# Attention in halves of 256 queries instead of chunks of 512, with two slots of turned probabilities and rings of eight for their parts

## The reference

```python
x = x + layernorm(attention(layernorm(x)))
# attention, per head h, weights = codes * scales (one scale per 32 rows):
q, k, v = xn @ Wq + bq, xn @ Wk + bk, xn @ Wv + bv      # [2048, 128] each
p = softmax(q @ k.T / sqrt(128))                        # [2048, 2048]
out += (p @ v) @ Wo[h]                                  # + bo
x = x + layernorm(moe(layernorm(x)))                    # top 2 of 8, 176 hidden
```

## Time and profile before

| | us |
|---|---|
| median of 3 runs | 2824.37 (2823.85 to 2857.05) |
| profiled execution, its own time | 2834.33 |
| span of the profiled execution | 2832.5 |
| mean granted TensorE clock | 0.943 of full |

### The profile page before, as it was taken

How to read it: one execution, slowest core, us unless ns; L and a number is a source line. 1 busy time by engine, 2 the same in 40 slices (tenths; PEclk the granted TensorE clock), 3 DMA queues, 4 the chain that set the end, 5 groups by cost and what they waited for, 6 DMA issues and landing times.

```text
span 2832.5 us, 36223 instructions
## 1 busy us (share of the span) xinstructions
PE 2300.4 (81%) x10540; PEld 1812.0 (64%) x10540; DVE 1730.0 (61%) x2335; ACT 1389.5 (49%) x2492; POOL 1546.7 (55%) x1376
## 2 busy tenths in 40 slices
PE   4878787878788887878787878878787878855998
PEld 3667575756667666757575666657566657644876
DVE  4666666657566666666675756666666657645443
ACT  2454454545454555555454545544554545433332
POOL 1455556656565555565565656555556655554433
PEclk8999999989999999999999999999999999977999
DMA  4445454445454454555454645445455455470000
GB/s 75 112 109 118 105 126 112 112 107 134 102 125 109 111 126 105 117 126 118 105 121 110 135 103 124 113 108 117 105 126 120 112 116 120 113 180 11 8 8 15
DMA packets 152845, 298.68 MB, mean 105 GB/s; under 512 B 44896, under 2 KB 87264, under 8 KB 152800
## 3 DMA queue, kind: packets, MB, share of 16 engines
q1 hardware_dynamic: 152800, 298.11, 46.0%
HBM read 27.43 MB, written 2.10 MB: 10 GB/s over the span
## 4 chain that ended last, share of the span: by engine, by line
issue 41%; POOL 37%; PE 13%; DVE 4%; SPq 3%; DMA 2%; ACT 1%; POOLq 1%; ACTq 0%; DVEq 0%
POOL pT L393 33%; PE ps_s L488 2%; PE ps_s L489 2%; PE ps_s L490 2%; SPq L301 2%; POOL codes L382 1%; DVE part_max L1000 1%; DMA acc<-in_L_attn_bo 1%; PE ps_a L488 1%; PE ps_a L747 1%; DVE probs L1013 1%; PE ps_a L490 1%; PE ps_a L489 1%; PE ps_a L749 1%; PE ps_a L750 1%
## 5 line engine op out<-in xcount | busy, mean ns | idle before, releaser
L393 POOL TENSOR_TENSOR pT<-pT,pT_hi 128x512 fp32r<-128x512 f32 x1024 | 1298.4, 1289 | 975.5 <-ACT pT_hi L802 974.5
L791 ACT ACTIVATE probs<-ps_s,shift 128x1024 f32<-128x1024 f32 x512 | 569.2, 1112 | 777.6 <-DVE shift L1006 777.6
L488 PE MATMUL ps_a<-pT_hi,v_hi 128*128 128x512 f32 x1024 | 449.7, 439 | 408.3 <-POOL pT L393 408.2
L1000 DVE TENSOR_REDUCE part_max<-ps_s 128x1 f32<-128x1024 f32 x512 | 619.2, 1209 | 262.3 <-PE ps_s L490 261.2
L1013 DVE STREAM_TRANSPOSE probs<-probs 128x1024 f32<-128x1024 f32 x512 | 632.2, 1235 | 195.5 <-ACT probs L791 195.5
L802 ACT ACTIVATE pT_hi<-pT 128x512 fp32r<-128x512 f32 x1024 | 606.1, 626 | 76.1 <-DMA pT<-probs 55.1
L488 PEld LDWEIGHTS ps_a<-pT_hi,v_hi 128*128 128x128 f32 x1024 | 196.5, 192 | 559.6 <-POOL pT L393 526.4
L488 PE MATMUL ps_s<-kT_hi,qT_hi 128*128 128x512 f32 x1024 | 419.1, 409 | 9.1 <-ACT probs L791 6.6
L489 PE MATMUL ps_s<-kT_lo,qT_hi 128*128 128x512 f32 x1024 | 416.4, 407 | 0.0
L490 PE MATMUL ps_s<-kT_hi,qT_lo 128*128 128x512 f32 x1024 | 413.1, 403 | 0.0
L489 PE MATMUL ps_a<-pT,v_hi 128*128 128x512 f32 x1024 | 409.0, 399 | 0.0
(11 more groups left out here) (159 smaller groups left out, 2915.9 us busy)
## 6 DMA issues: line engine op xcount, KB each, us to landing
pT<-probs SPq DMA_DIRECT2D x2048, 128.0 KB, 2.4
probs<-in_L_attn_x SPq DMA_DIRECT2D x4, 512.0 KB, 5.3
codes<-in_L_attn_wk_codes SPq DMA_DIRECT2D x16, 128.0 KB, 2.2
scales<-in_L_attn_wk_scales SPq DMA_DIRECT2D x64, 32.0 KB, 2.8
acc<-in_L_attn_bo SPq DMA_DIRECT2D x1, 2048.0 KB, 31.2
codes<-in_L_attn_wo_codes SPq DMA_DIRECT2D x16, 128.0 KB, 2.1
scales<-in_L_attn_wo_scales SPq DMA_DIRECT2D x64, 32.0 KB, 1.8
x<-in_L_attn_x SPq DMA_DIRECT2D x4, 512.0 KB, 7.5
```

The lines of the kernel that those rows point to most:

```text
L393: pool.tensor_tensor(tile, full(tile), full(pT_hi[:, k % RING, :]).rearrange("p (i q) -> p i q", i=Q4), ALU.subtract).then_inc(sm["p_lo_do ...
L488: nc.tensor.matmul(dst, lhs_hi, rhs_hi, start=first, stop=False)
L791: nc.scalar.activation(out, src, ACT.Exp, bias=shift[:, j % 2, r:r + 1], scale=SCALE, accum_out=sums[:, j % 2, r, g:g + 1])\
L1000: V.tensor_reduce(part_max[:, j % 2, r, g:g + 1], ps_s[:, pair_of(j, NG2 * r + g), :], AX.X, ALU.max)\
```

## The change

- Chunks of 512 queries become halves of 256 (8 per head, s; HQ = 256, RH = 2 rows). probs still has two slots, now of one half each.
- pT gets two slots (s % 2), each with all 16 key tiles of a half, and is no longer written by POOL. Low parts go to a ring of their own, pT_lo; pT_hi and pT_lo have eight places of two key tiles of 256 queries each (RING = 8). A position is such a pair; high and low parts still are 128 x 512 operations, but the value products have 256 columns, twice as many. HI_LAG = 2, PV_LAG = 6, out of 8 positions.
- turn_blocks is one step per half: 16 DMAs of 128 KB, of 64 rows of 2 KB where there were 32 rows of 4 KB. It waits for p_turned of the whole half and for POOL's low parts of two halves before.
- qT has two slots; q_proj, out_proj and add_out work on 256 queries, output three iterations on. The small statistics have four slots.
- V is made in two pieces of 1024 in the score banks (pair 0), in iteration 1; K in two pieces of 1024, in pairs 0 and 1. ring_of says which pair a score use has; around V's pieces two pairs are left for the scores.
- The x, normed, comes in through pT instead of probs. The experts' weights and x1 are loaded after the last turning DMAs have landed. wr is loaded and split, and `before` made, at the start, on POOL; pick and combT are prepared on POOL after the first norm of the expert stage, not before.

The core of the diff (orders of the engines' programs in an iteration are given as they are after):

```diff
-    RING = 4
+    RING = 8
     PAIRS = 3
-    USES = TPC * NG2
-    PV_LAG = 12
-    HI_LAG = 10
+    USES = RH * NG2
+    PV_LAG = 6
+    HI_LAG = 2
...
-        pT = sb("pT", [P, NG2, Q4, GT, P], f32r, att)
+        pT = sb("pT", [P, 2, NG2, Q4, GT, RH * 32], f32, att)
...
-        pT_hi = sb("pT_hi", [P, RING, CH], f32r, att)
+        pT_hi = sb("pT_hi", [P, RING, 2 * HQ], f32r, att)
+        pT_lo = sb("pT_lo", [P, RING, 2 * HQ], f32r, att)
...
+        def pair_at(h, s, pos, lag):
             if pos >= lag:
+                return half(h, s, -1) + (pos - lag,) if has(h, s, -1) else None
+            return half(h, s, -2) + (pos + PAIRS_KT - lag,) if has(h, s, -2) else None
...
+        def ring_of(s, use):
+
+            first = {1: 0, 2: 4, 3: 10, 4: 14, 5: 18, 6: 22, 7: 26, 0: 32}[s]
+            return (first + use + (1 if s == 2 and use > 1 else 0)) % PAIRS
...
+            def turn_blocks(h, s):
+
+                w = NH * h + s
+                wait(sp, "p_turned", USES * (w + 1))
                 sp.sem_inc(sm["turn_seen"], 1)
+                wait(sp, "p_lo_done", PAIRS_KT * (w - 1))
                 for i in range(Q4):
                     for b in range(Q4):
+                        src = probs[32 * i:32 * (i + 1), s % 2, :].rearrange("p (g j n) -> p g j n", g=NG2, j=Q4)
+                        dst = pT[32 * b:32 * (b + 1), s % 2, :, i, :, :].rearrange("p g t q -> p g (t q)")
+                        sp.dma_start(dst, src[:, :, b, :]).then_inc(pT_loaded[s % 2], 16)
...
+            def weighted_values(h, s, p):
+                w = NH * h + s
+                if p == 0:
+                    if has(h, s, 3):
+                        wait(pe, "q_lo", w + 4)
+                    wait(pe, "acc_done", w - 1)
...
+                wait(pe, "p_lo_done", PAIRS_KT * w + p + 1)
...
+                for t in range(2):
+                    k = 2 * p + t
+                    last = product3(out, v_hi[:, k, :], v_lo[:, k, :], hi[:, :, t, :], lo[:, :, t, :],
+                                    first=k == 0, last=k == KT - 1)
```

More of the change, by code:

```diff
@@ L401, in body @@
             def body(h):
[L402 to L407, removed]
+                inner, last = not isinstance(h, int) or 0 <= h < H, isinstance(h, int) and h == H - 1
+                for s in halves_of(h):
+                    for pos in range(PAIRS_KT):
+                        if inner and pos == 4:
+                            if s == 0 and not last:
@@ L618, in out_proj @@
+            def out_proj(h, s):
+                w = NH * h + s
+                wait(pe, "out_lo", w + 1)
+                if s == 0:
+                    wait(pe, w_ready["o"], h + 1)
+                for a in range(RH):
+                    rows = slice(a * P, (a + 1) * P)
+                    last = product3(ps_a[:, s % 2, a * D:(a + 1) * D], oT_hi[:, rows], oT_lo[:, rows],
                                     w_hi["o"][:, :, :].rearrange("p c n -> p (c n)"),
@@ L675, in _ @@
+                    if has(h, s, 1):
+                        scores(*nxt, 1, 1)
+                    key(6)
+                    key(7)
+                    if s == 1 and inner:
+                        v_proj(h, 1)
             heads(pe, body)
@@ L1031, in add_out @@
[L1031 to L1042 removed]
+                wait(dve, "total_done", w + 1)
@@ new lines, in body @@
+                    if s == NH - 1 and more:
+                        k_lo(h + 1, 0)
+                        k_lo(h + 1, 1)
+                    if more:
+                        part_of_max(*nxt, 0, 0)
+                    if inner:
+                        turn(h, s, 1, 1)
+                    if s == 2 and inner:
+                        value_lo(h, 1)
+                    if has(h, s, -3):
+                        add_out(*half(h, s, -3))
+                    if more:
+                        part_of_max(*nxt, 0, 1)
+                        row_shift(*nxt, 0)
@@ new lines, in body @@
+                    if inner:
+                        row_sums(h, s)
+                    if s == 4 and inner:
+                        bias_lo(h)
+                    if more:
+                        turn(*nxt, 0, 0)
+                    if has(h, s, 2):
+                        q_lo(*half(h, s, 2))
+                    if s == 1 and inner:
+                        value_lo(h, 0)
+                    if more:
+                        part_of_max(*nxt, 1, 0)
+                        turn(*nxt, 0, 1)
@@ new lines, in body @@
+                    if s == 4 and inner:
+                        add_bias(h)
+                    if more:
+                        part_of_max(*nxt, 1, 1)
+                        row_shift(*nxt, 1)
+                    if has(h, s, -2):
+                        out_lo(*half(h, s, -2))
+                    if more:
+                        turn(*nxt, 1, 0)
+                    if isinstance(h, int) and NH * h + s in range(HALVES - 4, HALVES + 4, 2):
+                        finish_chunk((NH * h + s - (HALVES - 4)) // 2)
```

680 lines of the change are left out of this document (302 added, 378 removed).

## The result

The changed kernel takes **2507.8 us** (median of 4 runs, 2505.9 to 2509.1) against 2828.9 for the kernel before on the same chip (2823.9 to 2857.1): ratio 0.885, 95% interval 0.879 to 0.891, so 11.5% faster. 2477 was forecast, 31 less.

What follows compares the result with a forecast made beforehand. Waits between engines round the single pT buffer were taken to bound the kernel, 153.6 us a head. Heads of 8 x 15.06 + 8.0 + 4.9 + 0.35 = 133.8 us, plus start, tail and expert stage, gave 2477 us; range 2415 to 2560.

Steps and rivals of the forecast that it cites:

- Ring: Attention loop: two pT slots and a low-part ring leave VectorE and ScalarE's loop, 15.1 us per 256 queries.
- What this loop needs of the others: DMAs, TensorE and POOL beside the attention loop: all fit, TensorE 119 us a head, nothing delays VectorE.
- Ends: Start, tail and expert stage: last turn at 2188, tail 27 us, then 268.6 us to a span of 2483.6.
- slack of 4.2: Turning DMAs of a half: landed at e+10.3 and needed at e+14.5, e being the iteration's first exponential; 4.2 us spare.
- Values through the score banks: V's two products in score banks delay maxima and scores by 8.0 us a head; K's two pieces add 4.9.
- DMA rows: Turning DMAs with 64 rows of 2 KB for 32 of 4 KB: no cost, sixteen still take 10.05 us.
- Rival (b): Turning DMAs: each row costs 19.6 ns as now, sixteen take 20.1 us; 3110 us, slower; chance 0.07.
- -2 for wr and pick: Start of the expert stage: VectorE's copies for wr and pick and POOL's memsets move away, saving 2 us.
- The factor 0.9965: Conversion from the profiled run to the median of plain runs, 0.35% lower: 2485.4 becomes 2477 us.
- (a): Attention loop: more waits than followed eat half the gains, 143 us a head, 2625 us; chance 0.18.
- (d): VectorE: something unseen, as contention with POOL's output, lengthens each maximum and turn by 0.34 us; no gain, 2825; chance 0.07.
- (c): TensorE's floor: V's and K's waits fall in VectorE's idle time, a head nears 127 us, 2370 us; chance 0.06.

Runs made afterwards that it cites:

- a2: Changed kernel, but a pT refill waits for TensorE's products of the half two before, in place of POOL's low parts; 2588.7 us, ratio 0.915.
- c3: b2 plus twenty matmuls that nobody reads, where TensorE stood behind K ahead of a head's first scores; 2439.8 us, ratio 0.861.
- d1: b2 with one pair's values and the output product ahead of a head's first scores, and TensorE's heads 1 to 14 written out; 2366.0 us, ratio 0.836.
- b2: Changed kernel with ScalarE's out_hi ahead of the exponential (1,0) and VectorE's q_lo behind the maximum of (1,0); 2425.7 us, ratio 0.855.
- c1: Changed kernel plus twelve matmuls that nobody reads ahead of TensorE's wait for out_lo, except in the K iteration; 2545.4 us, ratio 0.899.
- a4: Changed kernel with ScalarE's out_hi put ahead of the exponential (1,0); 2450.2 us, ratio 0.867.
- a1: Changed kernel with combT and pick taken back from 128 to 64 partitions; 2525.1 us.
- b4: Kernel before the change with only combT and pick widened from 64 to 128 partitions; 2814.7 us, ratio 0.994.

## Why the prediction was right, and where it was off

*Ring*: right. 15.06 reckoned, 14.89 measured, waits 0.73 and 1.54 where 0.8 and 1.5 were foretold. Worth -0.17 x 128 = -22 us. a2 shows that 81 us of the whole gain hang on the low parts' ring, which the step assumed and did not price apart from the slot.

*What this loop needs of the others*: this is the step that failed, in its sentence "Nothing of it reaches VectorE". It followed TensorE at full clock and with no loop around its code. Two terms were missing. The turn of TensorE's loop: the thirteen windows behind K are together 20.3 us longer than at 14.89 each (c3 shows the stand and d1 removes it, both in kernels that already had b2's orders; in the changed kernel itself the loop wasn't taken away). And half clock behind the stand ahead of out_lo: up to 0.65 us in most of the windows +5 and +7, 15 us in all (c1 and a4 each take it away); the bias's window has another 0.65, of which 0.35 was in the sum and the rest, 5 us, isn't settled, its clock being 1.00. A third is VectorE's own: the last head's bias window holds the first finish_chunk and is 21.65 us, 6 more, which *Ends* had forgotten. DMAs: 10.67 us in the median where 10.05 was taken, inside the slack of 4.2.

*Values through the score banks*: 8.0 and 4.9 reckoned, 8.26 and 5.36 measured, +11 us over the heads. Together: -22 + 20 + 20 + 6 + 11 = 35 us, and the last turn ended at 2224, not 2188.

*DMA rows*: no cost taken, and none on the path. Rival (b) is out; its price per row was wrong: twice the rows came with 2% more time for the quickest sixteen and 6% in the median.

*Ends*: tail 27.5 for 27. The expert stage was 14 us shorter than reckoned, the term "-2 for wr and pick" mis-sized: the diff's combT and pick were read as copies, not as the operands of a matmul in each of 44 groups (a1, b4). The factor 0.9965 from profile to median did not hold (profiled 2507.99, median 2507.77): +9. Sum: 2477 + 36 - 14 + 9 = 2508. That the forecast is off by 31 us only is in part luck: terms of some 66 us too little stood against 36 too much.

*Rivals*: (a) was right in kind, couplings that a hand-followed loop forgets, and far too dear; (d) shows nowhere (a maximum takes 1.205 us after and 1.209 before, a turn 1.236 and 1.235), and (c) only once VectorE's waits are taken away (b2).

## What to carry

Once the slow coupling is gone, ask of each engine's loop what its own turn costs: look for an "issue" wait once per pass at the same place, and compare passes inside the loop with those written out ahead of it and behind it. A wait that ends on a semaphore may hide one that would have been there anyway; an instruction without a wait, put in that place, tells the two apart. Look at every pass and not at the median alone: the few passes that are spared price the cost without any edit. Read a diff's shape changes for the matmuls that contract over them.

## What the hardware showed that I had not expected

- TensorE stands 2.3 to 3.25 us at nearly every turn of a loop of some 795 matmuls (13 of 13 times in c3, 12 of 13 in the changed kernel, 10 of 13 in a4, there up to 4.5 us), and mostly runs at half clock behind it (512 columns start 0.43 us apart, from 1141.9 to 1145.5 in the changed kernel and from 1101.8 to 1107.7 in b2), but not always (a stand of 3.00 us at 1413.1, with 0.23 us between starts behind it). With the heads written out, 14000 matmuls in a row, no such stand appears and the mean granted clock rises from 0.966 to 0.978.
- A stand of 1.74 us for out_lo was followed by half clock in some windows (0.41 us for 256 columns at 1108.5) and not in others (a stand of 1.75 us at 872.5, with 0.12 us between starts behind it).
- One matmul over 64 partitions among ones over 128 costs 0.4 us each time, in both kernels (0.98 or 0.97 us in place of 0.58 for the three starts around it).
- Rows of 1 KB that lie next to each other on both sides made no more packets than rows of 2 KB.
